# Layer 1 attention in a two-layer kernel: row maxima read 32 rows of each half of the array, with one set of split keys

## What is computed

```python
k = jnp.repeat(k, rep, axis=2)
v = jnp.repeat(v, rep, axis=2)
scores = jnp.einsum('bthd,bshd->bhts', q, k) / np.sqrt(HD)
causal = jnp.tril(jnp.ones((seq, seq), dtype=bool))
scores = jnp.where(causal[None, None], scores, -jnp.inf)
attn = jax.nn.softmax(scores, axis=-1)
out = jnp.einsum('bhts,bshd->bthd', attn, v)
```

## Time and profile before

| | us |
|---|---|
| median of 3 runs (lowest, highest) | 1468.04 (1463.27, 1469.57) |
| the profiled execution, its own time | 1474.87 |
| its span, first to last instruction | 1473.2 |
| PE busy (share of the span) | 1256.4 (85%) |
| PE weight loads busy | 758.2 (51%) |
| DVE busy | 982.3 (67%) |
| ACT busy | 691.6 (47%) |
| POOL busy | 381.6 (26%) |

### The profile page before, as it was taken

One profiled execution on the slowest core, in us unless ns is written; L12 is line 12 of the kernel. 1 busy time (PEld: TensorE's weight loads), 2 busy tenths in 40 slices (PEclk: granted clock), 3 DMA queues, 4 the chain that ended last, 5 costly groups with the idle time before them and its releaser, 6 DMA issues. The chain is left out here.

```text
span 1473.2 us, 20295 instructions
## 1 busy us (share of the span) xinstructions
PE 1256.4 (85%) x7132; PEld 758.2 (51%) x7132; DVE 982.3 (67%) x1750; ACT 691.6 (47%) x1319; POOL 381.6 (26%) x243
## 2 busy tenths in 40 slices
PE   4679999999999999589999976257988888789997
PEld 3444554545455454358888755123433343257886
DVE  4557646565755542579999956757677665448998
ACT  2232534444352434336666645213566557425664
POOL 0035465646656568000000000301111111020000
PEclk9799999999999999669999968657999979868999
DMA  3101202111120200046767400141222201111221
GB/s 107 42 15 36 50 16 60 24 50 30 39 44 16 46 16 29 4 97 148 156 147 158 96 1 0 15 115 30 49 62 61 53 20 35 29 43 60 96 90 29
DMA packets 51472, 81.54 MB, mean 55 GB/s; under 512 B 16749, under 2 KB 34453, under 8 KB 47445
## 3 DMA queue, kind: packets, MB, share of 16 engines
q1 hardware_dynamic: 51004, 79.40, 22.1%
q10 hardware_dynamic: 384, 1.05, 0.6%
HBM read 63.75 MB, written 5.68 MB: 47 GB/s over the span
## 5 line engine op out<-in xcount | busy, mean ns | idle before, releaser
L1369 PE MATMUL ps<-qA 128*128 128x512 f32 x960 | 254.1, 402 | 10.4 <-POOL qA L1479 10.4
L640 DVE TENSOR_REDUCE mraw<-ps 128x1 f32<-128x512 f32 (+3 forms) x304 | 183.2, 654 | 72.7 <-PE ps L520 41.3
L743 ACT ACTIVATE shared<-ps 128x512 f32<-128x512 f32 (+1 forms) x216 | 118.8, 565 | 227.5 <-PE ps L553 221.5
L1086 DVE TENSOR_REDUCE mraw<-ps 128x2 f32<-128x1024 f32 (+3 forms) x160 | 173.5, 1114 | 71.0 <-PE ps L994 47.8
L1141 ACT ACTIVATE shared<-ps 128x512 f32<-128x512 f32 (+2 forms) x320 | 154.7, 560 | 130.1 <-PE ps L1010 129.9
L1369 PEld LDWEIGHTS ps<-qA 128*128 128x128 f32 x960 | 183.5, 194 | 60.0 <-POOL qA L1479 12.1
L552 PE MATMUL ps<-qA,kH 128*128 128x512 f32 (+3 forms) x384 | 164.5, 438 | 8.2 <-DMA qB<-mT 6.5
L781 POOL TENSOR_TENSOR VP<-VP,shared 128x2048 f32<-128x2048 f32 (+3 forms) x40 | 129.7, 3242 | 66.1 <-ACT shared L743 64.0
L1433 ACT CAST qA<-shared 128x512 fp32r<-128x512 f32 x160 | 99.3, 620 | 87.3 <-DVE shared L1571 86.4
L1381 PE MATMUL ps<-qA,kH 128*128 128x512 f32 x480 | 135.5, 391 | 4.1 <-DVE qA L1495 4.0
L514 PE MATMUL ps<-kH,qA 128*128 128x512 f32 (+3 forms) x384 | 121.0, 380 | 17.1 <-DVE qA L630 8.9
(11 more groups left out here) (250 smaller groups left out, 1890.9 us busy)
## 6 DMA issues: line engine op xcount, KB each, us to landing
shared<-comb SPq DMA_DIRECT2D x92, 256.0 KB, 4.2
qB<-qA SPq DMA_DIRECT2D x16, 512.0 KB, 4.8
rB<-a0rec_dram SPq DMA_DIRECT2D x60, 128.0 KB, 2.9
shared<-comb SPq DMA_DIRECT2D x7, 1024.0 KB, 4.4
rB<-a1rec_dram SPq DMA_DIRECT2D x28, 128.0 KB, 2.7
e0wUp<-in_w SPq DMA_DIRECT2D x48, 64.0 KB, 4.6
qA<-q_split SPq DMA_DIRECT2D x24, 128.0 KB
q_split<-qA SPq DMA_DIRECT2D x4, 512.0 KB
```

Source lines behind the costliest of these rows:

```text
L640: nc.vector.tensor_reduce(out[:, h0:h0 + n_h, qt % 4], src, AX, ALU.max).then_inc(w_free, 1)
L743: nc.scalar.activation(probs(n)[:, hs[0]:hs[-1] + 1, lo:512], src, ACT.Exp, scale=scale)\
L1086: nc.vector.tensor_reduce(out[:, :, js[0]:js[-1] + 1, qt % 4], src, AX, ALU.max).then_inc(x_free, 1)
L1369: ins = nc.tensor.matmul(bank[0:M, :], w[par][:, at:at + M], h[:, cols], start=(r == 0), stop=(r == 2))
```

## The change

`TERMS` rows (32) in place of 64 are read by the max matmuls: rows 0 to 31 and rows 64 to 95. Row 32 is then outside what they read, and they take the keys of the scores. The zero-row key set is given up with its loads (DIRECT 12 for 16, LOADS 8 for 12) and with the clearing of kL0 and kL1. The mask matmuls and the score matmuls still read 64 rows. The order of all jobs is the same.

```diff
-        DIRECT, LOADS, STORES = 16, 12, 8
+        DIRECT, LOADS, STORES = 12, 8, 8
...
-        Q, kZero, kOne = split_buffers(k)
+        Q, K = split_buffers(k)
...
-                            rows = row_tile(i, 64)
+                            rows = row_tile(i, TERMS)
                             ins = nc.tensor.matmul(pair[:, i, slot * w:(slot + 1) * w],
                                                    Q[g % 3][rows, jj, qt * P:(qt + 1) * P],
-                                                   kZero[g % 3][rows, ch * 512:ch * 512 + w],
+                                                   K[g % 3][rows, ch * 512:ch * 512 + w],
                                                    start=(slot == 0), stop=not diagonal,
                                                    skip_group_check=True)
...
-                                               kOne[g % 3][rows, kt * P:(kt + 1) * P],
+                                               K[g % 3][rows, kt * P:(kt + 1) * P],
...
-                            ins = nc.gpsimd.memset(kOne[2][at:at + 1, :].bitcast(F32), 1.0)
+                            ins = nc.gpsimd.memset(K[2][at:at + 1, :].bitcast(F32), 1.0)
...
-                            for dst in (kZero, kOne):
-                                sp.dma_start(dst[g % 3][at:at + 2 * hd, :].bitcast(F32), src)\
-                                    .then_inc(in_ld[g % 3], 16)
+                            sp.dma_start(K[g % 3][at:at + 2 * hd, :].bitcast(F32), src).then_inc(in_ld[g % 3], 16)
...
-    kZero = [k.kL[0][:, :], k.kL[1][:, :], k.qA[1][:, 2, :]]
-    kOne = [k.kH[0][:, :], k.kH[1][:, :], k.qA[1][:, 3, :]]
-    return Q, kZero, kOne
+    K = [k.kH[0][:, :], k.kH[1][:, :], k.qA[1][:, 3, :]]
+    return Q, K
...
-            for sets in split_buffers(k)[1:]:
-                engine.dma_start(sets[b][at:at + 2 * hd, :].bitcast(F32), src).then_inc(k.a1_in[b], 16)
+            engine.dma_start(split_buffers(k)[1][b][at:at + 2 * hd, :].bitcast(F32), src).then_inc(k.a1_in[b], 16)
...
-                for stack in (k.kL[0], k.kL[1], k.kH[0], k.kH[1]):
+                for stack in (k.kH[0], k.kH[1]):
```

## The result

| | before | after |
|---|---|---|
| median of 4 runs (lowest, highest) | 1465.72 (1463.27, 1469.57) | 1569.87 (1560.84, 1582.16) |
| the profiled execution, its own time | 1474.87 | 1570.43 |
| its span | 1473.2 | 1568.7 |
| mean granted TensorE clock | 0.897 | 0.825 |

The changed kernel is slower, by a ratio of 1.0714 (95% interval 1.0635 to 1.0792), 104 us. The forecast was 1488 us, slower by 20, with a range up to 1508. So the direction was right and the size wrong by a factor of five. The time before is here the median of four executions, 2.3 us under the three of the table ahead of the prediction. The profiled execution of the kernel before took 9.2 us more than that median and the one of the changed kernel 0.6 us more, so the two profiles differ by 95.6 us where the medians differ by 104.

What follows compares the result with a forecast made beforehand. Bound: a loop in the layer 1 attention where ACT waits for score matmuls and their weight loads wait for ACT. Loads −5, loop +20 and earlier max jobs +5 gave +20 us, 1468.0 to 1488 us, range 1463 to 1508.

Steps and rivals of the forecast that it cites:

- Loads, −5: Start of the layer 1 attention: fewer key DMAs let maxima and first scores start sooner, −5 us, bounds 0 to 6.
- Memsets, 0: Before the stage: POOL clears two tiles instead of four, taken as 0, any gain bounded by 1.9 us.
- Rows read, "by itself nothing": Max matmuls: the same columns stream with half the rows, so no time is gained or lost by itself.
- Price of a change: Each geometry change between neighbouring matmuls costs 0.19 us, 0.14 into the masks, some 0.3 at the lower clock.
- The 30 max jobs ahead of step 4, +5: Max jobs before 1015 us, at low clock: the 19 with masks exceed PE's slack by some 0.25 us each, +5 us.
- The loop, +20: Attention, 1015 to 1240 us, PE and ACT awaiting each other in 2.89 us turns: geometry changes there add 20 us.
- The clock: Attention, 1015 to 1240 us: mean clock 0.91 means 18% of the time at 1.2 GHz, adding 2 us.
- rival 3: Attention: gaps or half-used rows hold the clock down another third of 225 us, 22 us on top, 1510 us; chance 0.12.
- The price of a slow step: Attention: a step at clock 0.50 takes 4.12 us in place of 2.89, 1.23 us more.

Runs made afterwards that it cites:

- experiment 1: The changed kernel, but the maxima read 64 rows again, with one key set and one geometry: 1456.5 us against 1468.0, ratio 0.9901.
- Experiment 2: The kernel before, with only the maxima reading 32 rows; two key sets, all loads and memsets kept: 1560.5 us, ratio 1.0617.
- experiment 5: The kernel of experiment 1, but maxima and scores read 33 rows, still in 64-row tiles: 1554.2 us, ratio 1.0586.
- experiment 3: The changed kernel, but masks and scores read 32 rows too, leaving out the maximum's subtraction and half of each mask: 1557.9 us, ratio 1.0609.
- experiment 4: The kernel before, plus a 2-column matmul of 32 rows ahead of each max job, adding geometry changes: 1556.3 us, ratio 1.0575.
- experiment 6: The kernel before, plus a 2-column matmul of 64 rows ahead of each max job, without geometry changes: 1478.5 us against 1465.1, ratio 1.0094.

## Why the prediction was wrong, point by point

- **Loads, −5.** Measured −3.6 (29.7 us from first issue to first score before, 26.1 after), and −3.9 in experiment 1. ACT's queue holds half of what it held, 4.5% of 16 engines for 8.5%. The mechanism was right. Maxima came 2.4 us sooner where 4.3 was worked out: the engine time saved does not all come out of the wait, since SP's 16 issues still take 22.03 us for 24.69, and the first max matmul now waits for the queries and no longer for the keys. Another 1.3 us came out of the way from there to the first score, where up to 1 was expected.
- **Memsets, 0.** Experiment 2 keeps all of them, and its first load is issued at 942.4 us, the changed kernel's at 943.5: nothing waited for them there.
- **Rows read, "by itself nothing".** This step failed. For the duration of a matmul at a given clock it holds (1106.77 to 1107.20 above is the usual 0.43 for 512 columns at 1.2 GHz). But the clock itself depends on the rows: experiment 5, 98 us.
- **Price of a change, 0.19 us (0.14 into the masks), 0.3 at the lower clock.** The mechanism was right and the size somewhat high. At 1.00 it is 0.09 into a max pair and 0.20 out of it, 0.145 on average. At the lower clock it is 0.13 in and 0.30 out. The step to the 32-row geometry does end the pulling ahead of weights. The rule of the Trainium skill (TensorEngine Tiling (Array Packing), Key Properties), that changing the tiling mode drains the engine, agrees with these rows.
- **The 30 max jobs ahead of step 4, +5.** First score to first exponential of step 4: 1008.96 − 969.58 = 39.4 us after, 37.5 before and 37.5 in experiment 1. So +1.9, under half of what was taken.
- **The loop, +20.** It can only be told apart roughly: experiments 3 and 5 have a main part of 343 and 341 us without added changes, the changed kernel 358 with them, at a slightly higher clock. That is 15 to 17 us or a little more. It is near the forecast, but by luck in part: that sum priced 76 jobs on a loop through ACT at a clock of 0.91, and these 15 us come from a stage where PE is busy 340 of 358 us, mostly at 0.50.
- **The clock, the term that failed.** It entered the sum as +2 and as rival 3: 22 us more, chance 0.12, with the argument "PE gets no idler, only slower". Rival 3 did name half-used rows, but nothing was set against them. That PE would not get idler came true (340 of 358 us busy, 221 of 258 before), and it did not help: taking it for a guard of the clock was the mistake. The main part fell from 0.86 to 0.54, and the part without added changes at 0.50 is 343 − 258 = 85 us longer. The price of a slow step was right, and only their number wrong: a clock of 0.86 means that 72% of 258 us ran at 1.00, 186 us or 64 turns of 2.89 us, and 64 × 1.23 is 79. In the profiles, 85 + 15 for the changes, + 6 after the last max job (38 us to the last exponential for 32), − 3.6 for the loads make 102. The rest of the program, which the change doesn't touch, was 7 us shorter, which gives the 95.6 between the profiles.

The row that could have warned was there: in the kernel before, come from a stretch (1182 to 1194 us above) in which the clock was 0.50 and PE busy for all 12 us. I read it as a price of a step and not as a sign that busy time does not buy the clock at once. The Trainium skill (TensorE: Matmul & The Clock Gate, HAM oscillation) advises against idle gaps. The fall near 1182 in the kernel before, in 2.39 us of waiting, agrees with it. In the changed kernel PE was busy 340 of 358 us at 0.54, and there that advice does not explain the low clock.

## What to carry to other kernels

Where a stage already slips to the lower clock now and then, price an edit of a matmul's shape by the clock first: naming fewer rows cost 98 us here in instructions that take no longer at a given clock, and changes of geometry between neighbours lowered the clock on top of their own price. Leaving zero rows in a matmul can be the cheaper choice: 64 rows, 31 of them zeros, gave 1456.5 us where 33 rows gave 1554.2. Keep the resource that the change saves (here the second key set and its loads) and give up the part of it that touches the shape; that version beats both kernels, the one before by 1%: 0.9901 (0.9867 to 0.9935).

## What was not expected of the hardware

- The granted clock goes with the rows that a matmul names: 0.89 at 64 rows and 0.51 at 33, with the same geometry, columns, order and nonzero data (experiments 1 and 5).
- It also falls with changes of geometry while maxima, masks and scores keep their 64 rows: 0.66 for 0.83 against the control (experiments 4 and 6). Of the 343 us for 269, 22 to 52 are the clock's, by estimate.
- PE was busy 183 of 186 us at 0.50 (1036 to 1222 in the changed kernel), while in the kernel before a clock that had fallen near 1182 was back after some 13 us.

What stays open: what it is in a change of geometry that holds the clock down, the time in which the array empties or something else; no run separates these. Also open is where the 7 us come from that experiment 1 gains beyond its loads: its clock in the main part was 0.89 for 0.86. Besides the first loads it also has fewer key loads within the stage and other values in row 32 of the keys that the maxima read, and no run separates these.
